# The state's part of the attention output: scaled after the product by ScalarE, instead of scaled queries by VectorE

## What is computed

```python
def step(carry, inp):
    c, n, m = carry
    qt, kt, vt, it, ft = inp
    m_t = jnp.maximum(ft + m, it)
    ie = jnp.exp(it - m_t)
    fe = jnp.exp(ft - m_t + m)
    c = fe[:, :, None, None] * c + ie[:, :, None, None] * jnp.einsum('bhd,bhe->bhde', vt, kt)
    n = fe[:, :, None] * n + ie[:, :, None] * kt
    num = jnp.einsum('bhde,bhe->bhd', c, qt)
    den = jnp.maximum(jnp.sum(n * qt, -1, keepdims=True), 1.0)
    return ((c, n, m_t), num / den)
```

## Time and profile before

| | us |
|---|---|
| median of 3 runs (lowest, highest) | 426.08 (424.91, 426.52) |
| the profiled execution, its time | 429.1 |
| its span, first to last instruction | 427.3 |
| TensorE busy (matmuls) | 375.8 |
| VectorE busy | 316.3 |
| ScalarE busy | 236.5 |
| GpSimd busy | 122.1 |
| mean granted clock of TensorE | 0.946 |

### The profile page before, as it was taken

One profiled execution on the slowest core, in us unless ns is written; L12 is line 12 of the kernel. 1 busy time (PEld: TensorE's weight loads), 2 busy tenths in 40 slices (PEclk: granted clock), 3 DMA queues, 4 the chain that ended last, 5 costly groups with the idle time before them and its releaser, 6 DMA issues.

```text
span 427.3 us, 11335 instructions
## 1 busy us (share of the span) xinstructions
PE 375.8 (88%) x3628; PEld 301.4 (71%) x3629; DVE 316.3 (74%) x1007; ACT 236.5 (55%) x634; POOL 122.1 (29%) x123
## 2 busy tenths in 40 slices
PE   8147999977999999999999999999989866879991
PEld 5117999723687787887878878778768733679990
DVE  7833777653658898878989788988789994658780
ACT  3734656611546767467684567655556912646550
POOL 2333543077001111103110120111031168334552
PEclk9566999996999999999999999999999989889997
DMA  7996223111799997876730000000002612323320
GB/s 171 392 316 237 68 71 59 38 43 44 151 179 188 187 176 184 180 181 153 185 92 0 0 0 0 0 0 0 2 2 60 228 62 83 117 69 90 98 67 1
DMA packets 57089, 44.57 MB, mean 104 GB/s; under 512 B 4063, under 2 KB 53857, under 8 KB 56673
## 3 DMA queue, kind: packets, MB, share of 16 engines
q1 hardware_dynamic: 54018, 38.14, 37.5%
q0 software_dynamic: 2752, 5.73, 4.8%
q10 hardware_dynamic: 288, 0.31, 0.4%
HBM read 17.98 MB, written 25.73 MB: 102 GB/s over the span
## 4 chain that ended last, share of the span: by engine, by line
PE 68%; ACT 9%; DVE 7%; issue 6%; DMA 4%; POOL 2%; another core or an unknown queue 1%; POOLq 0%; ACTq 0%; SPq 0%; DVEq 0%
PE bank L960 64%; ACT WVT L837 3%; DMA xn_rows<-XN 2%; POOL slots L531 2%; DMA XB<-xn_rows,IDX 1%; DVE ST L1508 1%; ACT XN L659 1%; PE bank L1086 1%; PE bank L1343 1%; ACT E L846 1%; ACT W1R L857 1%; DVE QS L2111 1%; PE bank L1244 1%; DMA XN<-slots 1%
## 5 line engine op out<-in xcount | busy, mean ns | idle before, releaser
L599 POOL TENSOR_TENSOR HS<-HS,MHALF 128x8 f32<-128x8 f32 x16 | 26.4, 1647 | 130.6 <-DVE HS L2161 130.6
L737 ACT ACTIVATE HT<-bank,W1R 128x128 f32<-128x128 f32 x138 | 40.6, 365 | 21.3 <-issue 11.0
L960 PE MATMUL bank<-XBT,W1R 128*128 128x128 f32 x368 | 51.9, 286 | 0.1
L960 PE MATMUL bank<-W,HT 128*128 x368 | 50.1, 280 | 0.5 <-issue 0.5
L960 PEld LDWEIGHTS bank<-XBT,W1R 128*128 128x128 f32 x368 | 47.2, 201 | 0.8 <-issue 0.4
L960 PEld LDWEIGHTS bank<-W,HT 128*128 128x128 f32 x368 | 46.1, 197 | 1.0 <-issue 0.7
L837 ACT ACTIVATE WVT<-bank,AC 128x128 f32<-128x128 f32 x128 | 36.5, 375 | 11.7 <-PE bank L960 11.3
L960 PE MATMUL bank<-MASKB,IDB 128*128 128x512 bf16 x111 | 35.7, 424 | 7.9 <-DVE CREDIT L1960 5.2
L801 ACT ACTIVATE QKT<-bank,COLS 128x512 f32<-128x512 f32 x32 | 22.0, 687 | 28.9 <-PE bank L960 28.9
L545 POOL DMA_INDIRECT XB<-xn_rows,IDX x23 | 22.6, 984 | 32.9 <-PE bank L1086 19.9
L584 POOL DMA_INDIRECT out<-YB,IDX x23 | 22.6, 983 | 25.8 <-DVE YB L1794 17.4
(11 more groups left out here) (377 smaller groups left out, 989.0 us busy)
## 6 DMA issues: line engine op xcount, KB each, us to landing
slots<-FILL SPq DMA_DIRECT2D x74, 258.0 KB
W<-w SPq DMA_DIRECT2D x2, 2048.0 KB, 12.3
XN<-slots SPq DMA_DIRECT2D x23, 129.0 KB
W<-w SPq DMA_DIRECT2D x1, 2064.0 KB, 7.9
y_rows<-YB SPq DMA_DIRECT2D x23, 64.0 KB
X<-x SPq DMA_DIRECT2D x4, 256.0 KB, 5.3
xn_rows<-XN SPq DMA_DIRECT2D x2, 512.0 KB, 8.8
XN<-X SPq DMA_DIRECT2D x1, 768.0 KB, 5.1
```

The source lines that it names most:

```text
L599: g.tensor_tensor(HS[:, 3, :], HS[:, 2, :], MHALF[:, 0:H], ALU.pow).then_inc(roots_ready, 1)
L737: ins = a.activation(HT[:, j % 2, c, :], bank[2 + j % 2][:, c * P:(c + 1) * P], ACT.Relu, bias=W1R[:, j % 2, F + c:F + c + 1])
L960: return t_.matmul(o, l, r, start=start, stop=stop, skip_group_check=True)
```

## The change

- The queries are no longer scaled. TensorE's `state_decays` (4 matmuls a chunk), ScalarE's `state_decays` (4 exponentials) and VectorE's `scale_q` are gone, with E1, QS, MINB, the semaphore qs_ready and the "state" uses of DM.
- `from_state` multiplies the plain queries QT with the state into the score banks SB. It therefore waits until VectorE's weigh of the odd heads has read them (`pt_ready`), and it stands earlier: ahead of projection s, in the last chunk of a sequence ahead of the next sequence's gates and of r. It runs the even heads first, then the odd, and gives `state_full` for each.
- ScalarE's new `lay_state` copies the 8 heads (128x65 each) from the score banks to the value banks with a scale per token and head, SINCE. `values` waits for it (`state_laid`) and adds to what it finds.
- SINCE comes from a third row block AG[:, 2] (one more operation 128x128 in `gate_rows`, one more transpose in `head_columns`). The state's 64 columns are now set to zero at a sequence's start (one more memset in `reset_state`), and in chunk 0 all 65 columns are multiplied where it was one.

```diff
@@ -251,9 +251,7 @@
         AC = sb("AC", [P, NC, H])
         EW = sb("EW", [P, NC, H])
         DEC = sb("DEC", [P, NC, NP_])
-        MINB = sb("MINB", [P, NC, NP_])
-        E1 = sb("E1", [P, NP_, P])
-        QS = sb("QS", [P, NP_, P])
+        SINCE = sb("SINCE", [P, NC, H])
         KW = sb("KW", [P, 2, H, HD])
         VX = sb("VX", [P, 2, H, HD + 1])
         RTH = sb("RTH", [P, HID])
@@ -372,7 +371,7 @@
             return pj_free[pj_bank(use)], b * (NPJ // 2) + pj_uses(b).index(use) // 2 + 2
 
 
-        DM_USES = ["carry", "columns", *(f"{what}{c}" for c in range(NC) for what in ("even", "odd", "state"))]
+        DM_USES = ["carry", "columns", *(f"{what}{c}" for c in range(NC) for what in ("even", "odd"))]
         NDM = len(DM_USES)
 
         def dm_full_at(b, use):
@@ -803,12 +802,12 @@
             def head_columns(b):
 
                 act.wait_ge(*dm_full_at(b, "columns"))
-                cols = DM[:, 0:2 * P].rearrange("p (i c r) -> p i c r", i=2, c=NC)
-                per_chunk = DM[:, 2 * P:2 * P + 2 * NC * NP_].rearrange("p (i c m) -> p i c m", i=2, c=NC)
+                cols = DM[:, 0:3 * P].rearrange("p (i c r) -> p i c r", i=3, c=NC)
+                per_chunk = DM[:, 3 * P:3 * P + NC * NP_].rearrange("p (c m) -> p c m", c=NC)
                 a.activation(AC[:, :, :], cols[:, 0, :, 0:H], ACT.Copy)
                 a.activation(EW[:, :, :], cols[:, 1, :, 0:H], ACT.Exp)
-                a.activation(MINB[:, :, :], per_chunk[:, 1], ACT.Copy)
-                a.activation(DEC[:, :, :], per_chunk[:, 0], ACT.Exp).then_inc(dm_free, 1)
+                a.activation(SINCE[:, :, :], cols[:, 2, :, 0:H], ACT.Exp)
+                a.activation(DEC[:, :, :], per_chunk, ACT.Exp).then_inc(dm_free, 1)
                 act.wait_ge(*dm_read_at(b, "columns"))
 
             def take(b, c, what):
@@ -837,14 +836,17 @@
                     ins = a.activation(DT[:, hf, m, :], DM[:, m * P:(m + 1) * P], ACT.Exp, bias=AC[:, c, h:h + 1])
                 ins.then_inc(dm_free, 1)
 
-            def state_decays(b, c):
+            def lay_state(b, c):
+
 
                 n = b * NC + c
-                act.wait_ge(qs_ready, n + 1)
-                act.wait_ge(*dm_full_at(b, f"state{c}"))
-                for m in range(4):
-                    ins = a.activation(E1[:, m, :], DM[:, m * P:(m + 1) * P], ACT.Exp, bias=MINB[:, c, m:m + 1])
-                ins.then_inc(dm_free, 1)
+                act.wait_ge(hv_read, n + 1)
+                for hf in range(2):
+                    act.wait_ge(state_full, 2 * n + hf + 1)
+                    for m in range(4):
+                        at, h = slice(m * 65, (m + 1) * 65), 2 * m + hf
+                        ins = a.activation(NB_[hf][:, at], SB[hf][:, at], ACT.Copy, scale=SINCE[:, c, h:h + 1])
+                    ins.then_inc(state_laid, 1)
 
             def first_state(b):
 
@@ -879,15 +881,18 @@
                 decays(b, c, 1)
                 if c > 1:
                     squares(b, c - 1)
+                if c == NC - 1 and not last:
+                    round_xc(b + 1)
                 if nxt:
                     take(*nxt, "o")
-                state_decays(b, c)
-                if c == NC - 1 and not last:
-                    round_xc(b + 1)
-                    head_gates(b + 1)
+                if c == NC - 1:
+                    lay_state(b, c)
+                    if not last:
+                        head_gates(b + 1)
                 if nxt:
                     take(*nxt, "r")
                 if c < NC - 1:
+                    lay_state(b, c)
                     take(*nxt, "s")
                 elif last:
                     layer_norm(1, 0)
@@ -1230,9 +1235,9 @@
 
                 pe.wait_ge(rows_ready, b + 1)
                 dst = dm_wait(b, "columns")
-                for i in range(2):
+                for i in range(3):
                     t_.transpose(dst[:, i * P:(i + 1) * P], AG[:, i, :], ident)
-                mm(dst[:, 2 * P:2 * P + 2 * NC * NP_], DECLQ[:, :], GM[:, :, :].rearrange("p i n -> p (i n)"))\
+                mm(dst[:, 3 * P:3 * P + NC * NP_], DECLQ[:, :], GM[:, :])\
                     .then_inc(dm_full, 1)
 
             def k_tokens(b, c):
@@ -1268,14 +1273,6 @@
                     ins = mm(DM[:, m * P:(m + 1) * P], SELQ[:, c, h * P:(h + 1) * P], M3[:, :], False, m == 3)
                 ins.then_inc(dm_full, 1)
 
-            def state_decays(b, c):
-
-                dm_wait(b, f"state{c}")
-                for m in range(4):
-
-                    ins = mm(DM[:, m * P:(m + 1) * P], SELQ[:, c, 2 * m * P + HD:2 * m * P + HD + P], M3[:, :])
-                ins.then_inc(dm_full, 1)
-
             def scores(b, c):
 
                 if c == 0:
@@ -1301,16 +1298,15 @@
                         pe.wait_ge(cs_copied, b + 1)
                     pe.wait_ge(*tr_read_at(b, f"u{c - 1}"))
 
-                pe.wait_ge(hv_read, n + 1)
-                pe.wait_ge(qs_ready, n + 2)
-                first = HD if c == 0 else 0
-                for m in range(4):
-                    for hf in range(2):
-                        rows = slice(hf * HD, (hf + 1) * HD)
-
+
+                pe.wait_ge(pt_ready, 2 * n + 3)
+                for hf in range(2):
+                    rows = slice(hf * HD, (hf + 1) * HD)
+                    for m in range(4):
                         for half in [slice(0, P)] if m == 0 else [slice(0, HD), slice(HD, P)]:
-                            mm(NB_[hf][half, m * 65 + first:(m + 1) * 65], QS[rows, m, half], CS[rows, m, first:],
-                               m == 0, False)
+                            ins = mm(SB[hf][half, m * 65:(m + 1) * 65],
+                                     QT[rows, m, c * P + half.start:c * P + half.stop], CS[rows, m, :])
+                    ins.then_inc(state_full, 1)
 
             def to_state(b, c):
 
@@ -1327,7 +1323,7 @@
 
                 pe.wait_ge(*pj_read_at(b, f"v{c}"))
                 for hf in range(2):
-                    pe.wait_ge(pt_ready, 2 * (b * NC + c) + hf + 2)
+                    pe.wait_ge(state_laid, 2 * (b * NC + c) + hf + 1)
                     for m in range(4):
 
                         for half in (slice(0, HD), slice(HD, P)):
@@ -1379,18 +1374,17 @@
                     down_out(b, 0)
                 if c < NC - 2:
                     k_tokens(b, c + 1)
+                if not more:
+                    from_state(b, c)
                 if not more and not last:
-                    state_decays(b, c)
                     head_gates(b + 1)
                 if last and c == 3:
                     early_logits(2)
-                elif more:
-                    state_decays(b, c)
                 if nxt:
                     project(*nxt, "r")
                 if more:
+                    from_state(b, c)
                     project(b, c + 1, "s")
-                from_state(b, c)
                 if c == 2 and not last:
                     head_z(b + 1)
                 if more:
@@ -2040,6 +2034,7 @@
 
             def reset_state():
 
+                v.memset(CS[:, :, 0:HD], 0.0)
                 v.memset(CS[:, :, HD:HD + 1], 1.0).then_inc(cs_ready, 1)
 
             def gate_scans(b):
@@ -2065,10 +2060,10 @@
                 do(v.tensor_scalar(MM[:, :], FL[:, 1, :], PAIR[:, 1:2], None, ALU.max))
                 did(v.tensor_copy(MHI[:, :], MM[:, :]))
                 did(v.tensor_scalar(AG[:, 1, :], AG[:, 0, :], MM[:, P - 1:P], None, ALU.subtract))
+                did(v.tensor_scalar(AG[:, 2, :], MM[:, :], PAIR[:, 1:2], -1.0, ALU.subtract, ALU.mult))
                 did(v.tensor_tensor(PAIR[:, 0:1], PAIR[:, 1:2], MM[:, P - 1:P], ALU.subtract))
                 step.settle()
-                v.tensor_tensor(GM[:, :, :], bc(PAIR[:, :], [P, 2, NC * NP_]),
-                                ROWM[:, :].unsqueeze(1).to_broadcast([P, 2, NC * NP_]), ALU.mult).then_inc(rows_ready, 1)
+                v.tensor_scalar(GM[:, :], ROWM[:, :], PAIR[:, 0:1], None, ALU.mult).then_inc(rows_ready, 1)
 
             def gate_copies(b):
 
@@ -2103,12 +2098,6 @@
                 dve.wait_ge(*dm_read_at(b, f"{('even', 'odd')[hf]}{c}"))
                 v.tensor_tensor(PT[:, hf, :, :].rearrange("p m t -> p (m t)"), SB[hf][:, :],
                                 DT[:, hf, :, :].rearrange("p m t -> p (m t)"), ALU.mult).then_inc(pt_ready, 1)
-
-            def scale_q(b, c):
-
-                n = b * NC + c
-                dve.wait_ge(*dm_read_at(b, f"state{c}"))
-                v.tensor_tensor(QS[:, :, :], QT[:, :, c * P:(c + 1) * P], E1[:, :, :], ALU.mult).then_inc(qs_ready, 1)
 
             def new_state(b, c):
 
@@ -2227,7 +2216,6 @@
                     last_addend(b)
                     weigh(b, 3, 1)
                     last_gate_scale()
-                    scale_q(b, 3)
                     early_choice()
                 if c == 3 and last:
                     update_x(b, 1)
@@ -2242,10 +2230,8 @@
                     shares(1, 0, EARLY)
```

(17 more changed lines are left out.)

## The result

| | before | after |
|---|---|---|
| median (lowest, highest), 4 runs each | 425.63 (424.91, 426.52) | 457.96 (457.26, 458.79) |
| ratio, 95% interval | | 1.0748 (1.0706 to 1.0789) |
| the profiled execution, its time / span | 429.1 / 427.3 | 457.26 / 455.4 |
| TensorE / VectorE / ScalarE busy | 375.8 / 316.3 / 236.5 | 395.4 / 310.0 / 248.4 |
| mean granted clock | 0.946 | 0.925 |

The kernel is slower by 7.5%, 32 us, where 434.0 (427 to 439) was forecast: the sign was right, the size four times too small. TensorE has fewer matmuls than before and is busy 20 us longer; that alone says that some of them have become longer.

What follows compares the result with a forecast made beforehand. TensorE was taken to set the pace, with a nearly as long VectorE loop in every chunk. Three passes +6.2, one transpose +0.15 and the last sequence +1.6 gave about 8 us on 426.08: 434.0 us, range 427.0 to 439.0.

Steps and rivals of the forecast that it cites:

- The length of from_state: TensorE's product of queries and state: 0.88 us from start to start, the new head order adding 0.
- chunk 0's 0.46: First chunk of a sequence: TensorE stands 0.8 us for VectorE's weigh, so values begin 0.46 us later.
- chunk 1: Second chunk of a sequence: from_state waits for VectorE's weigh, so values begin 0.09 us later.
- chunk 2: Third chunk: the weigh stands behind ScalarE's squares and VectorE's variance, TensorE stands 1.2 us, values begin 0.99 us later.
- chunk 3: Last chunk of a sequence: values begin 0.23 us earlier, because the scaled queries had been late here.
- The waits for the weigh: TensorE ahead of from_state, waiting for VectorE's odd-head weigh: 0.8, 0.9, 1.2 and 0.4 us in chunks 0 to 3.
- ScalarE's copies: Eight 128x65 copies from bank to bank take about 1.2 us, covered by other work, costing TensorE nothing.
- The end of a pass: VectorE, without slack and with 0.28 and 0.25 us added, decides: a pass 2.07 us longer, three passes +6.2.
- The last sequence: After the three passes: layer_norm behind ScalarE's copies delays VectorE's reduction and the kernel's end by 1.6 us.
- Waits for ScalarE gone: TensorE's waits for ScalarE's exponentials fall from 11.8 to under 3 us.
- long copies: Rival, chance 0.14: ScalarE's copies take 2.3 us, r is taken 1.1 later in chunk 3, +4.3, 438.3 us.
- faster: Rival, chance 0.09: VectorE's freed 0.69 us ends the weigh sooner, -1.0 us a sequence, 422.1 us.

Runs made afterwards that it cites:

- e9: Changed kernel with unread 512-column products filling TensorE's idle time ahead of the state product in chunks 0 to 2 (3, 4 and 4): 450.35 us, ratio 1.0529.
- e1: Changed kernel with from_state's old head order, even and odd heads in turn: 439.11 us, ratio 1.0278.
- e2: Kernel before with only from_state's head order changed, all even heads and then all odd: 438.51 us, ratio 1.0266.
- e8: e1 with four ScalarE copies of 130 columns instead of eight of 65 (wrong results, for timing only): 436.05 us, ratio 1.0172.
- e3: Kernel before plus only the added row block AG[:, 2], its transpose and the state memset, read by nothing: 428.01 us, ratio 1.0026.
- e4: e1 with VectorE's weigh of the odd heads put ahead of its other work of the step in chunks 0 to 2: 431.84 us, ratio 1.0102.
- e5: Changed kernel with four unread 512-column products filling TensorE's idle time ahead of the state product in chunk 2 only: 455.16 us, ratio 1.066.

## Why the prediction was wrong

- **The length of from_state: the step that failed.** "That its order is now by row half and not alternating isn't in any row; ... so 0 to 0.06 us more per chunk; I take 0." It is +0.84 in each of 16 chunks, 13.4 us of TensorE's time. The bound was drawn from `values`, whose matmuls fill all 128 rows and so say nothing of two halves in turn; it had a like count of matmuls in a like time and so looked near. Twenty-eight weight loads of 133 ns and as many matmuls of 226 ns fit into 0.88 us only because many are under way at once, on both halves. What lets them overlap was not asked, and an upper end of at least twice the length, 16 x 0.88 = 14 us, was left out of the range. Cost: 11.2 us (e9 against e1), and 11.6 in the kernel before (e2); in e9's pass chunks 1 to 3 have the 0.84 in full, and the end with chunk 0 only 0.52.
- **The clock: not in the prediction at all.** The earlier trace rows had 1.00 throughout, and I added waits of about a microsecond on TensorE without asking what they do to it. 7.6 us (after against e9). In e1 the same waits alone did nothing to it.
- **The rest: right in kind, a third too small.** e1 is the kernel that the prediction described: its median is 12.2 us above that of the kernel before in the same comparison (439.11 to 426.9), where 8 were forecast; the spans of the two profiled executions differ by 10.1 (437.4 to 427.3). By these traces, 0.67 of it lies ahead of the first values (forecast 0.15 and chunk 0's 0.46), 8.70 in the three passes (6.2), 0.73 behind. By parts of the second pass, e1 against before and in brackets the forecast: chunk 1 +0.24 (+0.09), chunk 2 +0.96 (+0.99), chunk 3 -0.17 (-0.23), chunk 0 and the end of the pass together +1.87 (+1.22); per pass 2.90 (2.07). The waits for the weigh were forecast as 0.8, 0.9, 1.2, 0.4 and are 0.68, 0.98, 1.14, 0.39.
- **ScalarE's copies: mis-sized.** 1.2 us taken, 1.72 to 1.76 measured, 0.21 from start to start. So r is read later at the end of a pass: VectorE reads it 1.06 us after the values begin (229.68 to 228.62 in e1), before 0.56 (224.57 to 224.01), +0.50. That is most of the 0.65 that chunk 0 and the end of the pass have above the forecast; e8 gives 0.3 of it back.
- **The end of a pass is VectorE's: right.** e3 gives +0.51 for the 0.28 and 0.25 of the forecast (0.28 and 0.27 measured), and the last transpose waits for OUT by 0.69 (1.02 in e1), forecast 0.6.
- **The last sequence: right in kind.** The reduction waits for the exponential (0.75 us, at 370.53 us of the changed kernel). From the last chunk 0 on, e1 has +0.73; the forecast was 1.6 less the 0.46 of chunk 0, 1.14. In the changed kernel the part behind the last values is 1.3 us shorter than before (86.4 against 87.7 in the profiled executions); I have no cause for it.
- **Waits for ScalarE gone: right,** 1.5 us left where under 3 was said. Of the rivals none was near; "long copies" (438.3) named a true effect: it took 2.3 us for the copies where the forecast took 1.2, and they last 1.74. For *faster* the prediction had VectorE without a gap in chunk 2, but its own show one of 0.30 us.
- The spans differ by 28.1 us and the medians by 32.3, because the profiled execution of before was 3.5 above its median and that of after 0.7 below.

## What to carry to other kernels

When an edit only reorders matmuls that use half of TensorE's rows, count it as a change of its length: in turn 28 took 0.88 us, by halves 1.72. Look for any stretch whose parts add up to more than it takes, and ask what lets them overlap. And a product that waits for an engine that reads its bank should have its cover looked for first: putting one VectorE operation earlier (e4) gave back half of what a pass had lost, 1.44 of 2.90 us.

## What the runs showed of the hardware

- Matmuls with a weight load each, on the upper and the lower 64 rows in turn, take 0.031 us each on average; all of one half and then all of the other 0.062 (0.88 and 1.72 us for 28, e1 and after). The series of one half has the same starts in both orders; in turn the two series run at the same time.
- In these runs the granted clock came down to 0.50 within the three loop passes only where TensorE had stood for 0.7 to 1.2 us and then ran the state product by halves (after, e5); the idle time alone (e1) and that product alone (e2, and e9 but for 0.47 us) did not bring it down. One fall lasts 3.4 us and costs about 1.5 (matmuls of 512 columns 0.43 instead of 0.23 apart). Which chunk gets it isn't explained by the idle time ahead of it: e5 fell behind 0.68 us in chunk 0, where the changed kernel, with the same 0.68 there, did not, and the changed kernel fell in chunk 1 of the first sequence alone, behind the same 0.98 as in the others.
- ScalarE's scaled copies of 128x65 from score bank to value bank start 0.21 us apart, those of 128x130 0.28 (1.14 for four): twice the width adds a third, so the number of copies counts for most.
